# Query norms in the exponential and the maximum, halves of squares on GpSimd, one sine product per rotation

## The chip, the cores and the metric

The kernel runs on one core of a Trainium2 chip. The core has five engines that run their own instruction streams in order and meet at semaphores: TensorE (PE; PEld is its weight load), VectorE (DVE), ScalarE (ACT), GpSimd (POOL) and SyncE (SP), which issues the DMAs. The metric is the device time of one execution in microseconds (us), less is better. The median of three runs before the change is 3862.86 us.

## The reference

The reference is a network of two layers on 16 sequences of 256 tokens with 128 features. Each layer has a modulation, an attention and a feed-forward part. The part that matters here is the feed-forward of the first layer, which is itself a stack of six local attentions with gated networks between them. Cut down, one of the six attentions is:

```
q, k, v = split(shift_tokens(x) @ Wqkv)          # 16 heads of 64
q = q / max(norm(q), 1e-12) * q_scale            # per token and head
k = k / max(norm(k), 1e-12) * k_scale
q = q*cos*scale + rotate_half(q)*sin*scale       # rotate_half: [-second half, first half]
k = k*cos/scale + rotate_half(k)*sin/scale
sim = 8 * q @ k.T    over windows of 32 queries and their 64 keys, masked
out = softmax(sim) @ v ;  x = x + out @ Wo
```

The norm of a query is one number per token and head. It can be applied to the query, or later to the whole row of scores of that token and head.

## The kernel before, in words

The six attentions are in `local_layers` (line 498). The loop over the layers holds a software pipeline over units. A unit is half of a tile of 128 tokens: 128 tokens by 8 heads (HG = 8, so PR = 4 pairs of heads), 4 units per sequence, 64 per layer, 384 in all. Every engine has a function `slot(u)` that does, for the current unit and for the units that lag one to five behind it, its part in a fixed order that is written out by hand; `u.has(n)` and `u.par(n)` speak of the unit that lags by n. Nothing plans the order at run time: an engine that waits holds up all that stands behind it.

One slot does, by engine:

- TensorE: projects keys (into PSUM bank PJ[1]) and queries (PJ[0]) of unit u, each as three passes of split floats (`three_passes`, lines 45 to 47). Then it transposes rotated keys and queries of unit u-2 (L637, into TB and TA), multiplies by Wo for u-5 (L696), transposes the weights of u-3 (TB) and the outputs of u-4 (TA). Then it projects the values of u into PJ[0] again, which needs that the queries there are rotated (`values`, line 662). Last come the mask (L736) and the scores (L743) of u-2 and the products with the values of u-3 (L756).
- ScalarE: the square of the queries (L876), the keys and queries of u-2 out of PSUM (L904, L907), the square of the keys (L876), the transposed weights (L915), Ln and Exp for the inverse norms (L921, L925), the outputs (L930), the values (L886), and eight exponentials of 64 columns for u-2 (L893), whose bias is the negative maximum per token and head.
- VectorE: the rotation of the queries (L1035 by the cosines over all 64 columns, L1036 and L1037 by the sines over 32 columns each, which swap the halves), the residual (L1071), the rotation of the keys, a Newton step for the inverse norms of u-1 (L1054, L1056, L1061), the maximum of the scores (L1083), the reciprocal of the sums (L1088), the sum of the squares of 16 heads of 64 columns (L1043), the normalisation of the outputs (L1095), and the lower bound of the sums (L1049).
- GpSimd: splits the input where due (L1215, L1218), adds the two parts of the rotated queries (L1239), multiplies rotated keys and queries of u-1 by their inverse norms (L1233, keys first), adds the two parts of the rotated keys (L1248).
- SyncE: the DMAs that lay the values out for the windows.

The lines that count for what follows:

```
PE: wait k_ready(u-2); transposes keys;  wait q_ready(u-2); transposes queries
ACT: wait proj_done, sum_done(u-1); Square
DVE: wait sq_done; rotate;   sums: tensor_reduce(raw, sq[128 x 16 x 64]) -> sum_done
POOL: t1 = t1 + t2 (queries); t1 *= rn (keys) -> k_ready; t1 *= rn (queries) -> q_ready; t1 = t1 + t2 (keys)
```

Of the kernel before, what the change touches and what calls it, by code (L numbers as in the profile page):

```python
# [7 lines left out]
ALU = mybir.AluOpType  # L8
# [454 lines left out]
def wait_chunk(eng, sem, u, per, r):  # L463
# [9 lines left out]
    "ln_done", "guess_done", "newton", "qadd_done", "q_ready", "k_ready", "qk_done", "qk_out", "score_done",  # L473
# [24 lines left out]
def local_layers(nc, g, w, lw):  # L498
# [5 lines left out]
    with ExitStack() as ctx:  # L504
# [14 lines left out]
        t2 = sb("t2", [128, 2, 2, HG, HD])  # L519
        raw = sb("raw", [128, 2 * HG, 2])  # L520
# [10 lines left out]
        pT = sb("pT", [128, 2, PR, 128])  # L531
        nm = sb("nm", [128, 2, 2, PR])
# [19 lines left out]
        with nc.Block() as block:  # L552
# [81 lines left out]
            def _(pe):  # L634
# [31 lines left out]
                def front(u):  # L666
# [4 lines left out]
                    if u.has(2):  # L671
# [6 lines left out]
                        pe.wait_ge(s.q_ready, u.count(1, 2, 1))  # L678
# [187 lines left out]
            def _(act):  # L866
# [4 lines left out]
                def squares(u, j):  # L871

                    act.wait_ge(s.proj_done, u.count(3, 0, 2 - j))
                    if u.was(1):
                        act.wait_ge(s.sum_done, u.count(1, 1, 1))
# [13 lines left out]
                def slot(u):  # L889
                    def weights(e):  # L890

                        for p in range(PR):
                            last = nc.scalar.activation(pb[:, u.par(2), p, e, :], SC[:, e, p * KEYS:(p + 1) * KEYS],  # L893
                                                        ACT.Exp, bias=nm[:, u.par(2), e, p:p + 1])
                        last.then_inc(s.exp_done, 1)
# [105 lines left out]
            def _(dve):  # L1001
# [12 lines left out]
                def make_tables(made):  # L1014

                    for t in range(2):
                        nc.vector.tensor_tensor(ctab[:, t, :, :], g.cbase[:, t, :, :], scb[:, :, :], ALU.mult)
                        nc.vector.tensor_tensor(stab[:, t, :, 0:32], g.sbase[:, t, :, 0:32], scb[:, :, 32:64], ALU.mult)
                        last = nc.vector.tensor_tensor(stab[:, t, :, 32:64], g.sbase[:, t, :, 32:64],
# [6 lines left out]
                def rotate(u, j):  # L1026

                    b, T = u.par(0), u.tile(0)
                    one, two = slice(0, 32), slice(32, 64)
                    x = PJ[j][:, :].rearrange("p (h d) -> p h d", h=HG)  # L1030
                    table = lambda t, c: t[:, T, j, c].unsqueeze(1).broadcast_to((128, HG, c.stop - c.start))
                    dve.wait_ge(s.sq_done, u.count(2, 0, 1 + j))
                    if u.was(2):
                        dve.wait_ge(s.qk_done, u.count(2, 2, 2 - j))
                    nc.vector.tensor_tensor(t1[:, b, j], x, table(ctab, slice(0, HD)), ALU.mult)  # L1035
                    nc.vector.tensor_tensor(t2[:, b, j, :, one], x[:, :, two], table(stab, one), ALU.mult)  # L1036
                    nc.vector.tensor_tensor(t2[:, b, j, :, two], x[:, :, one], table(stab, two),  # L1037
                                            ALU.mult).then_inc(s.rot_done, 1)

                def sums(u):  # L1040
                    if u.was(1):
                        dve.wait_ge(s.ss_done, u.count(1, 1, 1))
                    nc.vector.tensor_reduce(raw[:, :, 0], sq[:, :, :], AX.X, ALU.add).then_inc(s.sum_done, 1)  # L1043
# [7 lines left out]
                def newton(u):  # L1051
# [7 lines left out]
                    if u.was(3):  # L1059
                        dve.wait_ge(s.q_ready, u.count(1, 3, 1))  # L1060
# [3 lines left out]
                def slot(u, between=None):  # L1064
# [144 lines left out]
            def _(pool):  # L1209
# [11 lines left out]
                def slot(u):  # L1221
# [8 lines left out]
                    def normalise(j):  # L1230

                        here = t1[:, u.par(1), j]
                        nc.gpsimd.tensor_tensor(here, here, rn[:, u.par(1), j * HG:(j + 1) * HG].unsqueeze(2).broadcast_to(  # L1233
                            (128, HG, HD)), ALU.mult).then_inc(s.k_ready if j else s.q_ready, 1)

                    b = u.par(0)
                    if u.has(0):
                        pool.wait_ge(s.rot_done, u.count(2, 0, 1))
                        nc.gpsimd.tensor_tensor(t1[:, b, 0], t1[:, b, 0], t2[:, b, 0], ALU.add).then_inc(s.qadd_done, 1)  # L1239
                    if u.has(1):  # L1240
                        pool.wait_ge(s.rn_done, u.count(1, 1, 1))
                        pool.wait_ge(s.kadd_done, u.count(1, 1, 1))
                        normalise(1)
                        pool.wait_ge(s.qadd_done, u.count(1, 1, 1))
                        normalise(0)
                    if u.has(0):
                        pool.wait_ge(s.rot_done, u.count(2, 0, 2))
                        nc.gpsimd.tensor_tensor(t1[:, b, 1], t1[:, b, 1], t2[:, b, 1], ALU.add).then_inc(s.kadd_done, 1)  # L1248
# [1342 lines left out]
```

## Time and profile before

| | us |
|---|---|
| median of 3 runs | 3862.86 |
| lowest and highest run | 3859.14 and 3867.37 |
| span of the profiled execution | 3862.6 |
| TensorE busy in it | 3675.0 (95%) |
| VectorE busy | 3134.3 (81%) |
| ScalarE busy | 2886.4 (75%) |
| GpSimd busy | 2453.8 (64%) |

The profiled execution has no time of its own beside its span; the span stands 0.3 us from the median of the runs. The chain of work that ended last, as the page gives it, covers only the last few microseconds of the program and tells nothing of the local attention. The busy shares come from one profiled execution and are averages over all stages of the program; the local attention runs from about 250 to 3220 us of the span, with the gated network between its layers. In the rows below, times of the timeline are counted from the start of the span, and a bracket says how long the engine was idle before the row and what released it.

### The profile page before, as it was taken

The numbers are of one execution on the slowest core, as the hardware profiler recorded it, in microseconds if no ns is written. First come the engines' busy times: TensorE is split into PE (matmuls) and PEld (weight loads), VectorE is DVE, ScalarE is ACT, GpSimd is POOL, SyncE is SP. The second block draws the span as 40 slices with busy tenths as digits, with TensorE's granted clock in tenths as the row PEclk, the third lists the DMA queues.
The fourth block names the chain that finished last, engine by engine and source line by source line (L and its number), as shares of the span: only waits on it lengthen the run. The fifth ranks groups of instructions, "written<-read, shape, count | busy, mean of one in ns | idle before, by whom it ended". The sixth has DMA issues, their size and how long they took to land. (4 is left out here: it accounts for less than half of the span.)

```text
span 3862.6 us, 189335 instructions
## 1 busy us (share of the span) xinstructions
PE 3675.0 (95%) x70910; PEld 2943.1 (76%) x70910; DVE 3134.3 (81%) x9407; ACT 2886.4 (75%) x8517; POOL 2453.8 (64%) x2556
## 2 busy tenths in 40 slices
PE   7869999999999999999999999999999999899997
PEld 4558888688886788876888868888688886466665
DVE  7878888688887788877888878888788887666667
ACT  5758888478885688866888758888478885677775
POOL 3657777377774677755777647777377773454553
PEclk8979999999999999999999999999999999899998
DMA  1013333233332233332333323333233331100000
GB/s 48 1 56 83 81 82 81 60 81 81 81 81 69 72 81 80 82 83 58 83 80 82 90 52 81 81 81 82 60 81 81 81 81 46 36 1 0 0 0 28
DMA packets 305289, 245.99 MB, mean 64 GB/s; under 512 B 74485, under 2 KB 299860, under 8 KB 304340
## 3 DMA queue, kind: packets, MB, share of 16 engines
q1 hardware_dynamic: 305108, 243.72, 25.0%
q8 instruction: 96, 1.57, 0.2%
q14 instruction: 85, 0.70, 0.1%
HBM read 24.54 MB, written 2.12 MB: 7 GB/s over the span
## 5 line engine op out<-in xcount | busy, mean ns | idle before, releaser
L1233 POOL TENSOR_TENSOR wa_t<-wa_t,wa_rn 128x512 f32<-128x512 f32 x768 | 785.4, 1043 | 280.5 <-DVE wa_rn L1061 277.0
L893 ACT ACTIVATE wa_pb<-wa_sc,wa_nm 128x64 f32<-128x64 f32 x3072 | 672.5, 330 | 365.1 <-DVE wa_nm L1083 340.1
L1239 POOL TENSOR_TENSOR wa_t<-wa_t 128x512 f32<-128x512 f32 x384 | 496.1, 1292 | 409.7 <-DVE wa_t L1037 409.6
L1035 DVE TENSOR_TENSOR wa_t<-wa_pj,wa_ctab 128x512 f32<-128x512 f32 x768 | 527.0, 686 | 210.5 <-PE wa_ta L637 137.6
L45 PE MATMUL wa_pj<-lw_wqkv_high,wa_xhigh 128*128 128x512 f32 x1152 | 532.7, 462 | 36.3 <-DVE wa_t L1037 17.7
L876 ACT ACTIVATE wa_sq<-wa_pj 128x512 f32<-128x512 f32 x768 | 487.5, 636 | 60.4 <-PE wa_pj L47 57.8
L1248 POOL TENSOR_TENSOR wa_t<-wa_t 128x512 f32<-128x512 f32 x384 | 490.1, 1276 | 0.0
L47 PE MATMUL wa_pj<-lw_wqkv_high,wa_xlow 128*128 128x512 f32 x1152 | 459.9, 399 | 0.0
L46 PE MATMUL wa_pj<-lw_wqkv_low,wa_xhigh 128*128 128x512 f32 x1152 | 457.6, 397 | 0.9 <-issue 0.9
L1043 DVE TENSOR_REDUCE wa_raw<-wa_sq 128x16 f32<-128x1024 f32 x384 | 448.9, 1169 | 0.0
L696 PE MATMUL wa_ob<-wa_oT,lw_wo 128*128 128x128 f32 x3120 | 419.7, 278 | 2.7 <-DVE wa_on L1095 2.6
L756 PE MATMUL wa_ob<-wa_vv,wa_pT 64*32 64x65 f32 x24576 | 388.5, 227 | 25.1 <-issue 22.5
L696 PEld LDWEIGHTS wa_ob<-wa_oT,lw_wo 128*128 128x128 f32 x3120 | 382.4, 193 | 7.0 <-issue 5.1
L756 PEld LDWEIGHTS wa_ob<-wa_vv,wa_pT 64*32 64x32 f32 x24576 | 317.7, 105 | 37.2 <-issue 28.3
L2215 POOL TENSOR_TENSOR mq_pb<-mq_pb,mq_rs 128x256 f32<-128x256 f32 (+1 forms) x256 | 206.2, 826 | 219.7 <-DVE mq_rs L2360 219.7
L743 PE MATMUL wa_sc<-wa_kT,wa_qT 64*32 64x64 f32 x24576 | 327.9, 223 | 1.9 <-issue 1.8
L1036 DVE TENSOR_TENSOR wa_t<-wa_pj,wa_stab 128x256 f32<-128x256 f32 x768 | 316.9, 413 | 0.0
L1037 DVE TENSOR_TENSOR wa_t<-wa_pj,wa_stab 128x256 f32<-128x256 f32 x768 | 316.8, 413 | 0.0
L743 PEld LDWEIGHTS wa_sc<-wa_kT,wa_qT 64*32 64x32 f32 x24576 | 300.3, 105 | 2.8 <-issue 2.4
L1083 DVE TENSOR_REDUCE wa_nm<-wa_sc 128x8 f32<-128x512 f32 x384 | 265.5, 691 | 44.8 <-PE wa_sc L743 22.0
L45 PEld LDWEIGHTS wa_pj<-lw_wqkv_high,wa_xhigh 128*128 128x128 f32 x1152 | 217.7, 189 | 107.5 <-DVE wa_t L1037 29.7
L1095 DVE TENSOR_TENSOR wa_on<-wa_ob,wa_rs 128x512 f32<-128x512 f32 x384 | 261.3, 681 | 1.5
(291 smaller groups left out, 8631.5 us busy)
## 6 DMA issues: line engine op xcount, KB each, us to landing
wa_vv<-wa_vt SPq DMA_DIRECT2D x2304, 65.0 KB
wa_vv<-wa_vt SPq DMA_DIRECT2D x1152, 32.5 KB
lw_wqkv<-L_ffn_Wqkv SPq DMA_DIRECT2D x6, 1536.0 KB, 6.2
lw_xs<-yT SPq DMA_DIRECT2D x96, 64.0 KB
lw_fs<-yT SPq DMA_DIRECT2D x48, 128.0 KB
lw_xs<-yT SPq DMA_DIRECT2D x96, 63.8 KB
lw_fs<-yT SPq DMA_DIRECT2D x96, 63.8 KB
lw_wo<-L_ffn_Wo SPq DMA_DIRECT2D x6, 512.0 KB, 4.1
```

The costliest lines, as they stand in the source:

```text
L45: nc.tensor.matmul(out, lhs[0], rhs[0], start=start, stop=False)
L46: nc.tensor.matmul(out, lhs[0], rhs[1], start=False, stop=False)
L47: return nc.tensor.matmul(out, lhs[1], rhs[0], start=False, stop=stop)
L696: last = nc.tensor.matmul(OB[:, 0, Y0:Y0 + 128], wo[:, PR * h + j, :], oT[:, u.tile(5), PR * h + j, :], start=(j == 0), stop=(j == PR - 1) ...
L743: last = nc.tensor.matmul(SC[q, e, p * KEYS:(p + 1) * KEYS], qT[r, u.par(2), p, q], kT[r, h2, p, k0:k0 + KEYS], start=False, stop=True, sk ...
L756: last = nc.tensor.matmul(OB[q, e, p * VW:(p + 1) * VW], pT[r, u.par(3), p, q], vv[r, u.ring(3), n, p, :], start=True, stop=True, skip_gro ...
L876: nc.scalar.activation(sq[:, j * HG:(j + 1) * HG, :], PJ[j][:, :].rearrange("p (h d) -> p h d", h=HG), ACT.Square).then_inc(s.sq_done, 1)
L893: last = nc.scalar.activation(pb[:, u.par(2), p, e, :], SC[:, e, p * KEYS:(p + 1) * KEYS], ACT.Exp, bias=nm[:, u.par(2), e, p:p + 1])
L1035: nc.vector.tensor_tensor(t1[:, b, j], x, table(ctab, slice(0, HD)), ALU.mult)
L1233: nc.gpsimd.tensor_tensor(here, here, rn[:, u.par(1), j * HG:(j + 1) * HG].unsqueeze(2).broadcast_to((128, HG, HD)), ALU.mult).then_inc(s. ...
L1239: nc.gpsimd.tensor_tensor(t1[:, b, 0], t1[:, b, 0], t2[:, b, 0], ALU.add).then_inc(s.qadd_done, 1)
L1248: nc.gpsimd.tensor_tensor(t1[:, b, 1], t1[:, b, 1], t2[:, b, 1], ALU.add).then_inc(s.kadd_done, 1)
```

## The change

Four things are changed, all in `local_layers`:

- The queries are no longer multiplied by their inverse norm. GpSimd's product for them goes, and with it the semaphore q_ready; TensorE waits for the addition (qadd_done) instead. The inverse norm now is the scale operand of the eight exponentials, and VectorE multiplies the negative maximum by it in an instruction of its own, after a wait for the maximum (peak_done).
- GpSimd adds the first and the second 32 squares of each head (into the new tile sh), and VectorE sums the 32 results instead of 64 squares. This addition stands first in GpSimd's slot, behind the split of the input; it waits for both squares of the unit, and signals half_done, for which the next squares and the sum wait.
- The rotation multiplies by the sines in one instruction of 64 columns, without the swap. The table of sines is laid out swapped for it.
- GpSimd's addition does the swap: two instructions of 32 columns per head in place of one of 64, for queries and for keys.

```diff
-                        pe.wait_ge(s.q_ready, u.count(1, 2, 1))
+                        pe.wait_ge(s.qadd_done, u.count(1, 2, 1))
...
-                        act.wait_ge(s.sum_done, u.count(1, 1, 1))
+                        act.wait_ge(s.half_done, u.count(1, 1, 1))
...
-                                                        ACT.Exp, bias=nm[:, u.par(2), e, p:p + 1])
+                                                        ACT.Exp, bias=nm[:, u.par(2), e, p:p + 1],
+                                                        scale=rn[:, u.par(2), 2 * p + e:2 * p + e + 1])
...
-                        nc.vector.tensor_tensor(stab[:, t, :, 0:32], g.sbase[:, t, :, 0:32], scb[:, :, 32:64], ALU.mult)
-                        last = nc.vector.tensor_tensor(stab[:, t, :, 32:64], g.sbase[:, t, :, 32:64],
+                        nc.vector.tensor_tensor(stab[:, t, :, 32:64], g.sbase[:, t, :, 0:32], scb[:, :, 32:64], ALU.mult)
+                        last = nc.vector.tensor_tensor(stab[:, t, :, 0:32], g.sbase[:, t, :, 32:64],
...
-                    nc.vector.tensor_tensor(t1[:, b, j], x, table(ctab, slice(0, HD)), ALU.mult)
-                    nc.vector.tensor_tensor(t2[:, b, j, :, one], x[:, :, two], table(stab, one), ALU.mult)
-                    nc.vector.tensor_tensor(t2[:, b, j, :, two], x[:, :, one], table(stab, two),
-                                            ALU.mult).then_inc(s.rot_done, 1)
+                    nc.vector.tensor_tensor(t1[:, b, j], x, table(ctab), ALU.mult)
+                    nc.vector.tensor_tensor(t2[:, b, j], x, table(stab), ALU.mult).then_inc(s.rot_done, 1)
...
-                    nc.vector.tensor_reduce(raw[:, :, 0], sq[:, :, :], AX.X, ALU.add).then_inc(s.sum_done, 1)
+                    dve.wait_ge(s.half_done, u.count(1, 0, 1))
+                    nc.vector.tensor_reduce(raw[:, :, 0], sh[:, :, :], AX.X, ALU.add).then_inc(s.sum_done, 1)
...
-                        dve.wait_ge(s.q_ready, u.count(1, 3, 1))
+                        dve.wait_ge(s.exp_done, u.count(2, 3, 2))
...
-                        nc.vector.tensor_reduce(nm[:, u.par(2), :, :], SC[:, :, 0:PR * KEYS].rearrange(
-                            "p e (a b) -> p e a b", a=PR), AX.X, ALU.max, negate=True).then_inc(s.mx_done, 1)
+                        nc.vector.tensor_reduce(mx[:, u.par(2), :, :], SC[:, :, 0:PR * KEYS].rearrange(
+                            "p e (a b) -> p e a b", a=PR), AX.X, ALU.max, negate=True).then_inc(s.peak_done, 1)
+                        dve.wait_ge(s.peak_done, u.count(1, 2, 1))
+                        nc.vector.tensor_tensor(nm[:, u.par(2), :, :], mx[:, u.par(2), :, :],
+                                                rn[:, u.par(2), 0:HG].rearrange("p (a e) -> p e a", e=2),
+                                                ALU.mult).then_inc(s.mx_done, 1)
...
+                    def turned(j):
+
+                        for to, of in ((one, two), (two, one)):
+                            here = t1[:, b, j, :, to]
+                            last = nc.gpsimd.tensor_tensor(here, here, t2[:, b, j, :, of], ALU.add)
+                        return last
+
                     if u.has(0):
+                        pool.wait_ge(s.sq_done, u.count(2, 0, 2))
+                        if u.was(1):
+                            pool.wait_ge(s.sum_done, u.count(1, 1, 1))
+                        nc.gpsimd.tensor_tensor(sh[:, :, :], sq[:, :, one], sq[:, :, two], ALU.add).then_inc(s.half_done, 1)
                         pool.wait_ge(s.rot_done, u.count(2, 0, 1))
-                        nc.gpsimd.tensor_tensor(t1[:, b, 0], t1[:, b, 0], t2[:, b, 0], ALU.add).then_inc(s.qadd_done, 1)
+                        turned(0).then_inc(s.qadd_done, 1)
                     if u.has(1):
                         pool.wait_ge(s.rn_done, u.count(1, 1, 1))
                         pool.wait_ge(s.kadd_done, u.count(1, 1, 1))
-                        normalise(1)
-                        pool.wait_ge(s.qadd_done, u.count(1, 1, 1))
-                        normalise(0)
+                        here = t1[:, u.par(1), 1]
+                        nc.gpsimd.tensor_tensor(here, here, rn[:, u.par(1), HG:2 * HG].unsqueeze(2).broadcast_to(
+                            (128, HG, HD)), ALU.mult).then_inc(s.k_ready, 1)
                     if u.has(0):
                         pool.wait_ge(s.rot_done, u.count(2, 0, 2))
-                        nc.gpsimd.tensor_tensor(t1[:, b, 1], t1[:, b, 1], t2[:, b, 1], ALU.add).then_inc(s.kadd_done, 1)
+                        turned(1).then_inc(s.kadd_done, 1)
```

## Rows read from the trace of the kernel before

**Rows 1.** The page: busy time, share of the span and instructions of each engine.

```profile
PE 3675.0 (95%) x70910; PEld 2943.1 (76%) x70910; DVE 3134.3 (81%) x9407; ACT 2886.4 (75%) x8517; POOL 2453.8 (64%) x2556
```

**Rows 2.** Windows: one stretch inside the local attention, busy us per engine, clock.

```profile
core 0: us, PE busy (x) PEld busy (x) DVE busy (x) ACT busy (x) POOL busy (x), PEclk, DMA share, GB/s
840.00:1160.00 320.00, 320.00 (x8152) 278.99 (x8158) 285.53 (x730) 273.43 (x829) 241.72 (x243) 1.00 0.33 81
```

**Rows 3.** The sum of squares, once per unit, in that stretch: min/median/max ns.

```profile
L1043 DVE TENSOR_REDUCE wa_raw<-wa_sq x49: 1165/1166/1170, 839.5 to 1155.3; 128x16 f32<-128x1024 f32 x49
```

**Rows 4.** Timeline of one unit: start, us, engine, line, out<-in, count, idle before.

```profile
902.61 0.49 PE L45 MATMUL wa_pj<-lw_wqkv_high,wa_xhigh 128*128 128x512 f32 x1
...
904.60 0.69 DVE L1083 TENSOR_REDUCE wa_nm<-wa_sc 128x8 f32<-128x512 f32 x1
...
905.33 1.75 ACT L893 ACTIVATE wa_pb<-wa_sc,wa_nm 128x64 f32<-128x64 f32 x8 [0.93 <-DVE wa_nm L1083]
...
906.28 0.59 PEld L637 LDWEIGHTS wa_tb<-ident,wa_t 128*128 128x128 f32 x4
...
906.92 0.65 ACT L876 ACTIVATE wa_sq<-wa_pj 128x512 f32<-128x512 f32 x1
...
907.66 0.69 DVE L1035 TENSOR_TENSOR wa_t<-wa_pj,wa_ctab 128x512 f32<-128x512 f32 x1 [0.48 <-ACT wa_sq L876]
...
908.27 0.41 DVE L1036 TENSOR_TENSOR wa_t<-wa_pj,wa_stab 128x256 f32<-128x256 f32 x1
...
908.35 0.68 ACT L876 ACTIVATE wa_sq<-wa_pj 128x512 f32<-128x512 f32 x1
908.60 0.41 DVE L1037 TENSOR_TENSOR wa_t<-wa_pj,wa_stab 128x256 f32<-128x256 f32 x1
...
909.07 0.49 PE L45 MATMUL wa_pj<-lw_wqkv_high,wa_xhigh 128*128 128x512 f32 x1
...
910.39 0.16 DVE L1054 TENSOR_TENSOR wa_rc<-wa_rg 128x16 f32<-128x16 f32 x1
910.58 0.18 DVE L1056 SCALAR_TENSOR_TENSOR wa_rc<-wa_rc,wa_ss 128x16 f32<-128x16 f32 x1
...
911.05 2.05 POOL L1233 TENSOR_TENSOR wa_t<-wa_t,wa_rn 128x512 f32<-128x512 f32 x2 [0.66 <-DVE wa_rn L1061]
...
911.68 1.75 ACT L893 ACTIVATE wa_pb<-wa_sc,wa_nm 128x64 f32<-128x64 f32 x8 [0.82 <-DVE wa_nm L1083]
...
912.87 0.59 PEld L637 LDWEIGHTS wa_tb<-ident,wa_t 128*128 128x128 f32 x4
```

**Rows 5.** Timeline near a layer's start: a square and the rotation that waited.

```profile
1284.22 0.65 ACT L876 ACTIVATE wa_sq<-wa_pj 128x512 f32<-128x512 f32 x1
...
1284.90 0.69 DVE L1035 TENSOR_TENSOR wa_t<-wa_pj,wa_ctab 128x512 f32<-128x512 f32 x1 [0.96 <-ACT wa_sq L876]
```

**Rows 6.** Waits over the whole program: us in total, times, longest us.

```profile
PEld wa_pj L45 <- DVE wa_t L1037: 29.7, 27, 2.9
...
PE wa_pj L45 <- issue: 12.2, 4, 3.3
```

**Rows 7.** ScalarE by form (total us, mean ns), and a timeline of four with both operands.

```profile
L915 ACT ACTIVATE wa_pT<-wa_tb 128x512 f32<-128x512 f32 x384 | 230.8, 601 | 26.0 <-PE wa_tb L637 18.7
L1540 ACT ACTIVATE la_col<-la_b,la_vec 128x512 f32<-128x512 f32 x24 | 16.5, 687 | 10.3 <-PE la_b L1438 10.3
L1582 ACT ACTIVATE la_row<-la_b,la_neg,la_rstd 128x128 f32<-128x128 f32 x32 | 12.0, 462 | 0.0
L1597 ACT ACTIVATE aT<-la_b,la_vec 128x512 f32<-128x512 f32 x8 | 6.2, 778 | 8.8 <-PE la_b L1429 8.8
...
124.51 1.50 ACT L1582 ACTIVATE la_row<-la_b,la_neg,la_rstd 128x128 f32<-128x128 f32 x4
```

**Rows 8.** GpSimd by form: total us and mean ns of one.

```profile
L1239 POOL TENSOR_TENSOR wa_t<-wa_t 128x512 f32<-128x512 f32 x384 | 496.1, 1292 | 409.7 <-DVE wa_t L1037 409.6
...
L1218 POOL TENSOR_TENSOR wa_xlow<-lw_xs,wa_xhigh 128x128 fp32r<-128x128 f32 x192 | 88.1, 459 | 15.0
```

More of the change, by code:

```diff
@@ L472 @@
     "xs_ready", "proj_done", "session", "sq_done", "ss_done", "sum_done", "rn_done", "rot_done",
-    "ln_done", "guess_done", "newton", "qadd_done", "q_ready", "k_ready", "qk_done", "qk_out", "score_done",
+    "ln_done", "guess_done", "newton", "qadd_done", "k_ready", "half_done", "peak_done", "qk_done", "qk_out", "score_done",
     "mx_done", "exp_done", "pT_done", "pT_out", "pv_done", "rs_done", "norm_done", "oT_done", "oT_out",
@@ L519, in local_layers @@
         t2 = sb("t2", [128, 2, 2, HG, HD])
+        sh = sb("sh", [128, 2 * HG, HD // 2])
         raw = sb("raw", [128, 2 * HG, 2])
@@ L531, in local_layers @@
         pT = sb("pT", [128, 2, PR, 128])
+        mx = sb("mx", [128, 2, 2, PR])
         nm = sb("nm", [128, 2, 2, PR])
@@ L1028, in rotate @@
                     b, T = u.par(0), u.tile(0)
-                    one, two = slice(0, 32), slice(32, 64)
                     x = PJ[j][:, :].rearrange("p (h d) -> p h d", h=HG)
-                    table = lambda t, c: t[:, T, j, c].unsqueeze(1).broadcast_to((128, HG, c.stop - c.start))
+                    table = lambda t: t[:, T, j, :].unsqueeze(1).broadcast_to((128, HG, HD))
                     dve.wait_ge(s.sq_done, u.count(2, 0, 1 + j))
@@ L1228, in slot @@
                         split_input(0, u.sequence(32, u.lead + 1, 32), u.sequence(4, u.lead + 1, 1))
[L1230 to L1234, printed above, removed]
                     b = u.par(0)
+                    one, two = slice(0, HD // 2), slice(HD // 2, HD)
+                    def turned(j):
[3 more added lines that the diff above has]
+                        return last
                     if u.has(0):
+                        pool.wait_ge(s.sq_done, u.count(2, 0, 2))
+                        if u.was(1):
+                            pool.wait_ge(s.sum_done, u.count(1, 1, 1))
+                        nc.gpsimd.tensor_tensor(sh[:, :, :], sq[:, :, one], sq[:, :, two], ALU.add).then_inc(s.half_done, 1)
                         pool.wait_ge(s.rot_done, u.count(2, 0, 1))
-                        nc.gpsimd.tensor_tensor(t1[:, b, 0], t1[:, b, 0], t2[:, b, 0], ALU.add).then_inc(s.qadd_done, 1)
+                        turned(0).then_inc(s.qadd_done, 1)
                     if u.has(1):
```

## The prediction, made before the changed kernel ran

> **What bounds the kernel now.** The first view is the table of engines on the page: TensorE is busy 95% of the span and VectorE 81% [rows 1]. The share of busy time averages over stages, so the second view is a stretch inside the local attention, 840 to 1160 us: TensorE is busy 320.00 of 320 us at full granted clock, while VectorE, ScalarE and GpSimd keep 10 to 25% idle [rows 2]. In that stretch one unit (128 tokens by 8 heads) takes (1155.3 - 839.5) / 48 = 6.58 us [rows 3], and there are 384 units, 2526 us of the 3862.6. So the question is what one unit costs.
>
> TensorE has no gap, but the reader must not stop there: all engines run in order, and a ring of work goes round once per unit beside TensorE's own queue. In the timeline of one unit [rows 4] it reads: TensorE begins the value projection V (902.61); scores follow, and VectorE begins their maximum at 904.60, 1.99 later; the eight exponentials begin at 905.33, 0.73 later; ScalarE, in order, begins the square of the next unit's queries at 906.92, 1.59 later; VectorE rotates those queries from 907.66, of which 0.65 is the square and 0.03 the hand-over (1284.22 + 0.65 = 1284.87, rotation at 1284.90 [rows 5]); the rotation ends at 908.60 + 0.41 = 909.01, 1.35 later; V of the next unit, which overwrites the queries' bank, begins at 909.07, 0.06 later. Necessary work in the ring: 1.99 + 0.73 + 1.59 + 0.68 + 1.35 + 0.06 = 6.40 us, against a period of 6.58. **The ring has only 0.18 us of slack.** Whatever is added to it beyond that is paid in every unit, however busy TensorE is; what is taken from VectorE outside it is worth nothing.
>
> **The change part by part.**
>
> *Reduction of squares.* The sum over 1024 columns (1.17 us, [rows 3]) becomes one over 512, about 0.63. It lies behind the reciprocal, in no link of the ring: VectorE gains 0.54 us of idleness per unit, which I price at nothing. Only where TensorE waits for a rotation (29.7 us in 27 places over the whole program [rows 6]) could an earlier VectorE show, and there too the queue in front of the rotation isn't the sum but the square.
>
> *Rotation.* Three products (start to start 0.60, 0.33, then 0.41 to its end, 1.35 in all) become two of 512 columns: 0.60 + 0.69 = 1.29. It is in the ring: -0.06.
>
> *Norm of queries in the maximum.* The maximum now goes to a tile of its own, then waits for its own semaphore, and a product of 8 columns makes the bias. No row has this product; the nearest is the chain of small operations in the Newton step, 910.39 to 910.58, 0.19 per link with its wait [rows 4]. Bounds: 0.10 (half a link) and 0.30 (one and a half). I take 0.19. The norm itself was made a unit earlier, so it isn't waited for. Queued behind on VectorE are the reciprocal, the sum and the normalisation, which have slack; who waits for it is ScalarE with the exponentials. In the ring: +0.19.
>
> *Norm of queries in the exponential.* Eight exponentials of 64 columns get a second operand per partition, the scale. Three rows of 512 columns from PSUM give its price: no such operand 0.601 us, bias alone 0.687, bias and scale 0.778 [rows 7], so the scale adds 0.091. That is the duration of one; what matters is the distance of starts. Now it is (1.75 - 0.33) / 7 = 0.203 us. With both operands on 128 columns from PSUM, four in a row take 1.50 us with 0.462 each: (1.50 - 0.462) / 3 = 0.346 [rows 7]. From 128 to 64 columns comes off what the columns cost: (0.778 - 0.462) / 384 = 0.82 ns each, 0.053 us. So 0.293 with both, and 8 x 0.293 = 2.34 against 1.59 before: +0.75. Bounds: 0 (the operand's read hides behind the seven neighbours) and 8 x 0.13 = 1.0. I take the duration's own difference, 8 x 0.091 = +0.73, since it needs no step from 128 to 64 columns.
>
> The Trainium skill, "ScalarE: Activation LUTs", section "What ACT_TABLE_LOAD costs", says that each per-partition pointer operand adds about 93 ns to an ACTIVATE and that neighbours overlap by about 93 ns. The first agrees with the 0.091 of the rows and would make the term 0.74 and the sum 4106 us. The second would put today's starts 0.24 apart, where the trace has 0.203; the measurement decides.
>
> *GpSimd.* Removed: the product of the query norm, 1.00 from start to start. Added: the halves of the squares, 512 columns, 1.25. The two additions of 1.27 become four of 256 columns; the rows have 0.459 at 128 and 1.292 at 512 [rows 8], so some 0.74 each, 0.70 from start to start. Per unit: 1.25 + 4 x 0.70 + 1.00 = 5.05, and with the split of the input 5.5 on average and 6.0 at most: below the period, so its load doesn't bind. Its order might: the key norm now stands behind the half addition, which waits for both squares. Square of keys to its end, +0.06, +1.25, +1.40, +1.04: keys are ready 3.75 after it; today it was 909.03, which gives 912.78 against TensorE's need at 912.87 [rows 4]. In the longer ring the key square ends 0.08 after V begins (V - 0.06 - 1.29 - 0.03 + 1.46), the keys are ready at V + 3.83 and TensorE asks at V + 3.80: late by hundredths, in front of a stretch in which TensorE waits 0.68 for the rotation anyway. Price nothing; with halves that don't shrink (1.29 each) it would be the bound, see below. The queries, on the other hand, are ready over 3 us earlier, which nobody waits for.
>
> **The sum.** New ring: 1.99 + 0.73 + 0.19 + (1.59 + 0.73) + 0.68 + 1.29 + 0.06 = 7.26 us. It passes the 6.58 of TensorE's queue, so the period becomes 7.26, +0.68. Not all 384 units pay: the first few of each layer stand in stalls of other causes (projections that wait up to 3.3 us for TensorE's own issue [rows 6]) and the last few have no next unit to square. I take 58 of 64, an estimate: 6 x 58 x 0.68 = 237, and 0.9 us longer once per layer at its end, of which half is hidden, 3. Span 3862.6 + 240 = 4103. The median of the runs, 3862.86, stands within 0.3 us of the profiled span, so nothing is converted: **4103 us**, 6% slower. TensorE is late next: it waits 0.68 us per unit for the rotation, some 9% of the loop.
>
> **Rivals.**
>
> 1. *The scale costs nothing between neighbours.* For it: neighbours overlap already by 0.13 each. Against: the 0.346 with both operands, also between neighbours. Ring 7.26 - 0.73 = 6.53, under 6.58, so TensorE's queue stays the bound: 3860, no change.
>
> 2. *Faster, by VectorE's relief.* Same condition, decided at a scaled start distance of at most 0.203 + (6.58 - 6.53) / 8 = 0.21 us; then VectorE's 0.6 us of new idleness can reach the 27 places where TensorE waits for a rotation. Price at most 29.7: 3833. Against it is the same row as above, and that those waits follow the squares.
>
> 3. *The scale costs about half* (starts 0.245 apart): ring 6.90, +0.32, 348 x 0.32 = 111: 3974. For it: sharing of the two operand reads; no row shows it.
>
> 4. *GpSimd becomes the bound.* The ring over two units through the key square, half addition, keys, transposes, V and exponentials is, from the weight load of the key transposes to V 906.28 to 909.07, 2.79; to the maximum 1.99; to the exponentials 0.92; to the next square 2.32; to the key square's end 906.92 to 909.03, 2.11; to the keys 3.75: 13.88 us, 6.9 per unit. From 1.0 us per half addition on it passes 7.26, and from 1.14 on GpSimd's own load does. With 1.29 each that load is 1.25 + 5.0 + 1.0 + 0.43 = 7.7 per unit: 348 x 1.1 = 383, 4245 us. Against: 459 ns at 128 columns shows that cost falls with the columns; for: rows of 32 columns with gaps are in no row.
>
> **How the numbers follow.** Forecast 0.79 (its own range 4050 to 4150, from the bounds 0.10 and 0.30 of the small product, and 0.27 to 0.31 of the start distance); rival 4 with its milder forms 0.08; rival 3 0.05; rival 1 0.04; rival 2 0.04. The range reaches 3990 to 4175, which leaves out the two rivals without the operand's cost and the outer part of 3 and 4. A measurement of this kernel can tell about 0.2% from no change; so faster 0.05, same 0.04, slower 0.91.
>
> **What would show it.** In the profile after: exponentials of some 420 ns, eight of them in 2.4 to 2.5 us instead of 1.75; unit period 7.2 to 7.3; TensorE with about 0.6 to 0.7 us of idleness per unit, in front of V or of the transposes just before it, released by the rotation or by ScalarE; ScalarE's idleness before the exponentials reduced; the sum near 0.63 us and much more idleness on VectorE; GpSimd halves of 0.7 us. The forecast is wrong if exponentials stay near 0.2 apart, if the period is set by the wait for GpSimd's keys, or if TensorE's granted clock, 1.00 in the loop, falls because of the new gaps.

## The result and the profile after

The changed kernel takes 4538.45 us (median of 4 runs, 4535.65 to 4540.83) against 3864.08 us (4 runs, 3859.14 to 3867.37): a ratio of 1.1747, 95% interval 1.1731 to 1.1764. It is 17.5% slower. The prediction had the sign, 4103 us and a range up to 4175: it saw little more than a third of the loss. Of the executions reported below, three were in a slower state (one of g1_dummy512 at 5691 us, two of g2_dummy_memset at 7034 and 8564) and enter no ratio.

The page of the kernel after, its engines and two of its costliest groups, against [rows 1]; the last row is the group of the exponentials before:

```profile
span 4538.8 us, 189966 instructions
...
PE 3865.4 (85%) x70910; PEld 2896.4 (64%) x70910; DVE 3412.0 (75%) x9023; ACT 3122.3 (69%) x8517; POOL 2648.0 (58%) x3324
...
L895 ACT ACTIVATE wa_pb<-wa_sc,wa_nm,wa_rn 128x64 f32<-128x64 f32 x3072 | 949.1, 414 | 836.7 <-DVE wa_nm L1087 836.7
...
L1242 POOL TENSOR_TENSOR wa_t<-wa_t 128x256 f32<-128x256 f32 x1536 | 1087.5, 730 | 0.0
...
L893 ACT ACTIVATE wa_pb<-wa_sc,wa_nm 128x64 f32<-128x64 f32 x3072 | 672.5, 330 | 365.1 <-DVE wa_nm L1083 340.1
```

ScalarE's exponentials waited 837 us for the bias, against 340 before. The odd number is VectorE's: 3412 us busy against 3134 before, though the columns of its sum were halved and its rotation has one instruction less. The groups of VectorE by form say where, total us and mean ns of one:

```profile
L1057 DVE SCALAR_TENSOR_TENSOR wa_rc<-wa_rc,wa_ss 128x16 f32<-128x16 f32 x384 | 245.2, 639 | 13.2
L1044 DVE TENSOR_REDUCE wa_raw<-wa_sh 128x16 f32<-128x512 f32 x384 | 241.9, 630 | 0.0
L1062 DVE SCALAR_TENSOR_TENSOR wa_rn<-wa_rc,wa_rg 128x16 f32<-128x16 f32 x384 | 233.9, 609 | 21.3
L1087 DVE TENSOR_TENSOR wa_nm<-wa_mx,wa_rn 128x8 f32<-128x8 f32 x384 | 193.6, 504 | 13.2
...
L1055 DVE TENSOR_TENSOR wa_rc<-wa_rg 128x16 f32<-128x16 f32 x384 | 85.1, 222 | 10.9 <-ACT wa_rg L928 10.9
```

The sum is 0.63 us as forecast. But two products of the Newton step, on 16 columns, have grown from 0.18 us in [rows 4] to 0.64 and 0.61, and the new product of 8 columns takes 0.50. The timeline of one unit shows what they have in common (compare [rows 4]):

```profile
1008.59 1.28 POOL L1249 TENSOR_TENSOR wa_sh<-wa_sq 128x512 f32<-128x512 f32 x1 [3.31 <-ACT wa_sq L878]
...
1009.71 0.20 DVE L1055 TENSOR_TENSOR wa_rc<-wa_rg 128x16 f32<-128x16 f32 x1
1009.83 1.42 POOL L1242 TENSOR_TENSOR wa_t<-wa_t 128x256 f32<-128x256 f32 x2
1009.94 0.65 DVE L1057 SCALAR_TENSOR_TENSOR wa_rc<-wa_rc,wa_ss 128x16 f32<-128x16 f32 x1
...
1010.72 0.56 DVE L1062 SCALAR_TENSOR_TENSOR wa_rn<-wa_rc,wa_rg 128x16 f32<-128x16 f32 x1
...
1011.20 0.68 DVE L1084 TENSOR_REDUCE wa_mx<-wa_sc 128x8 f32<-128x512 f32 x1
1011.36 1.04 POOL L1256 TENSOR_TENSOR wa_t<-wa_t,wa_rn 128x512 f32<-128x512 f32 x1
...
1011.91 0.51 DVE L1087 TENSOR_TENSOR wa_nm<-wa_mx,wa_rn 128x8 f32<-128x8 f32 x1
...
1012.36 1.41 POOL L1242 TENSOR_TENSOR wa_t<-wa_t 128x256 f32<-128x256 f32 x2
...
1012.46 2.47 ACT L895 ACTIVATE wa_pb<-wa_sc,wa_nm,wa_rn 128x64 f32<-128x64 f32 x8 [2.22 <-DVE wa_nm L1087]
...
1016.06 0.68 DVE L1038 TENSOR_TENSOR wa_t<-wa_pj,wa_stab 128x512 f32<-128x512 f32 x1
...
1016.93 0.48 PE L45 MATMUL wa_pj<-lw_wqkv_high,wa_xhigh 128*128 128x512 f32 x1
```

L1057 begins at 1009.94 and ends at 1010.59; GpSimd's first half addition began at 1009.83 and lasts 0.73, to 1010.56. L1062 ends at 1011.28; the second half addition ended at 1011.24. L1087 ends at 1012.42; the key norm ended at 1012.40. Each of the long VectorE instructions ends 0.02 to 0.04 us after a GpSimd instruction. Counted over all 384 units: L1057 begins while GpSimd runs in 373 and then takes 0.653 us (median), and 0.175 in the other 11; L1062 0.650 in 366 and 0.175 in 18; L1087 0.510 in 378 and 0.168 in 6. The reduction L1044, the rotations and L1100, which have at most one input in SBUF, keep their durations.

### The profile page after: what moved, and what is told of

It reads as the page before. It is cut to its first block and busy times, and to the rows that moved or that the text cites. A ratio compares the mean times of both kernels' runs of the same rounds, so it can differ in the third digit from the quotient of the medians.

```text
span 4538.8 us, 189966 instructions
## 1 busy us (share of the span) xinstructions
PE 3865.4 (85%) x70910; PEld 2896.4 (64%) x70910; DVE 3412.0 (75%) x9023; ACT 3122.3 (69%) x8517; POOL 2648.0 (58%) x3324
## 5 line engine op out<-in xcount | busy, mean ns | idle before, releaser
L895 ACT ACTIVATE wa_pb<-wa_sc,wa_nm,wa_rn 128x64 f32<-128x64 f32 x3072 | 949.1, 414 | 836.7 <-DVE wa_nm L1087 836.7
L1249 POOL TENSOR_TENSOR wa_sh<-wa_sq 128x512 f32<-128x512 f32 x384 | 494.2, 1287 | 1091.4 <-ACT wa_sq L878 1091.4
L1242 POOL TENSOR_TENSOR wa_t<-wa_t 128x256 f32<-128x256 f32 x1536 | 1087.5, 730 | 0.0
L639 PE MATMUL wa_tb<-ident,wa_pb 128*128 128x128 f32 x1536 | 247.2, 284 | 383.0 <-ACT wa_kT L907 380.9
L1038 DVE TENSOR_TENSOR wa_t<-wa_pj,wa_stab 128x512 f32<-128x512 f32 x768 | 522.0, 680 | 0.0
L639 PEld LDWEIGHTS wa_tb<-ident,wa_pb 128*128 128x128 f32 x1536 | 162.3, 141 | 448.8 <-ACT wa_kT L907 226.2
L1256 POOL TENSOR_TENSOR wa_t<-wa_t,wa_rn 128x512 f32<-128x512 f32 x384 | 400.9, 1044 | 71.3 <-DVE wa_rn L1062 30.1
L758 PE MATMUL wa_ob<-wa_vv,wa_pT 64*32 64x65 f32 x24576 | 348.0, 228 | 29.5 <-issue 26.2
L758 PEld LDWEIGHTS wa_ob<-wa_vv,wa_pT 64*32 64x32 f32 x24576 | 284.3, 105 | 33.7 <-issue 32.6
L1084 DVE TENSOR_REDUCE wa_mx<-wa_sc 128x8 f32<-128x512 f32 x384 | 260.5, 678 | 1.2 <-PE wa_sc L745 0.8
L1100 DVE TENSOR_TENSOR wa_on<-wa_ob,wa_rs 128x512 f32<-128x512 f32 x384 | 259.3, 675 | 1.5
```

What stands on the lines that cost most here:

```text
L758: last = nc.tensor.matmul(OB[q, e, p * VW:(p + 1) * VW], pT[r, u.par(3), p, q], vv[r, u.ring(3), n, p, :], start=True, stop=True, skip_gro ...
L1038: nc.vector.tensor_tensor(t2[:, b, j], x, table(stab), ALU.mult).then_inc(s.rot_done, 1)
L1242: last = nc.gpsimd.tensor_tensor(here, here, t2[:, b, j, :, of], ALU.add)
L1249: nc.gpsimd.tensor_tensor(sh[:, :, :], sq[:, :, one], sq[:, :, two], ALU.add).then_inc(s.half_done, 1)
```

## The experiments

**Theory A.** A VectorE instruction whose two tensor inputs both lie in SBUF doesn't get through while a GpSimd instruction with SBUF inputs runs; it waits for that instruction's end. (A tile lies in SBUF or in PSUM; the kernel makes the first by `sb` and the second by `ps`.) **Rival B.** The products are long for a reason of VectorE's own (semaphores, code, order). A third theory, for the other part of the loss, is the prediction's: the scale operand costs 0.73 us per unit in the ring.

All runs in one table: the links of the ring of the prediction, us, each a mean over 228 units (38 in the loop of each of the six layers), worked out from the timelines; then the median time and its ratio to before. V is the start of TensorE's value projection; the columns follow the ring from there to the next V. In VectorE's order the Newton step stands right in front of the maximum, so a Newton product that is held shows in "V to max", and the product of the maxima shows in "to exp".

| kernel | V to max | to exp | to square | to rotation | rotation | to V | period | time | ratio |
|---|---|---|---|---|---|---|---|---|---|
| before | 2.00 | 0.73 | 1.65 | 0.77 | 1.35 | 0.08 | 6.58 | 3864 | 1 |
| predicted ring | 1.99 | 0.92 | 2.32 | 0.68 | 1.29 | 0.06 | 7.26 | 4103 | |
| after | 2.74 | 1.26 | 2.32 | 0.69 | 1.29 | 0.15 | 8.45 | 4538 | 1.175 |
| f1_rc_psum | 2.22 | 1.12 | 2.32 | 0.69 | 1.29 | 0.15 | 7.80 | 4309 | 1.116 |
| f2_mx_psum | 2.74 | 0.92 | 2.32 | 0.69 | 1.29 | 0.15 | 8.12 | 4418 | 1.144 |
| f3_both_psum | 2.22 | 0.93 | 2.33 | 0.69 | 1.29 | 0.15 | 7.62 | 4238 | 1.097 |
| f4_scale0 | 2.75 | 1.26 | 1.59 | 0.70 | 1.29 | 0.15 | 7.74 | 4266 | 1.105 |
| e4_order | 1.92 | 1.15 | 2.32 | 0.69 | 1.29 | 0.15 | 7.52 | 4197 | 1.087 |
| f6_order_mx | 1.91 | 0.94 | 2.33 | 0.69 | 1.29 | 0.15 | 7.31 | 4129 | 1.068 |
| f7_order_mx_scale0 | 1.98 | 0.94 | 1.59 | 0.71 | 1.29 | 0.14 | 6.65 | 3885 | 1.005 |
| e6_norm_only | 1.91 | 1.15 | 2.32 | 0.69 | 1.35 | 0.10 | 7.53 | 4213 | 1.091 |
| e7_half_only | 2.87 | 0.72 | 1.59 | 0.72 | 1.35 | 0.09 | 7.34 | 4133 | 1.071 |
| e8_sine_only | 1.99 | 0.73 | 1.66 | 0.77 | 1.29 | 0.14 | 6.57 | 3857 | 0.999 |
| g1_dummy512 | 2.94 | 0.72 | 1.59 | 0.72 | 1.35 | 0.08 | 7.42 | 4155 | 1.075 |
| g2_dummy_memset | 2.00 | 0.73 | 1.65 | 0.77 | 1.35 | 0.08 | 6.58 | 3863 | 1.000 |

### Where the inputs lie

**f1_rc_psum**: the Newton step's tile in PSUM.

```diff
-                    b = u.par(1)
+                    b, rc = u.par(1), rs_tail if u.tail else PJ[1][:, 0:16]
+                    if not u.tail:
+                        dve.wait_ge(s.rot_done, u.count(2, 0, 2))
...
+                    if u.was(2):
+                        pe.wait_ge(s.rn_done, u.count(1, 2, 1))
                     project(u, PJ[1], 1)
```

> The kernel after, with the Newton step's small tile rc in PSUM (in the keys' bank, free by then) instead of SBUF; all instructions and their order stay. Theory A (a VectorE instruction with two SBUF inputs waits until GpSimd's running instruction ends): the two Newton products that read rc fall from 0.64 and 0.61 us to about 0.2 each, since they now read one SBUF tile. The maximum starts 0.6 us earlier, but its product then falls on GpSimd's key norm (1.04 us) and waits for nearly all of it, so that the unit keeps all but 0.1 to 0.2 us: 4470 to 4510 us, and the product grows from 0.50 to 0.9 to 1.0 us. Rival B (the long products are the engine's own, from semaphores, code or the order of the work): the products stay at 0.6 us, 4538 us or a little more.

Measured: 4308.66 us, ratio 1.116 (1.1141 to 1.1179). The two products that now read one SBUF tile fell to 0.18 and 0.17 us: theory A, not B. (In a layer's last unit the tile stays in SBUF; 378 of 384 units read PSUM.) The time fell by 230 us, much more than expected, because the product of the maxima didn't grow to 0.9 us but shrank, from 504 to 370 ns on the mean. Two units show how:

```profile
1005.53 1.43 POOL L1247 TENSOR_TENSOR wa_t<-wa_t 128x256 f32<-128x256 f32 x2
1005.67 0.18 DVE L1062 SCALAR_TENSOR_TENSOR wa_pj<-wa_pj,wa_ss 128x16 f32<-128x16 f32 x1
...
1005.89 0.17 DVE L1067 SCALAR_TENSOR_TENSOR wa_rn<-wa_pj,wa_rg 128x16 f32<-128x16 f32 x1
...
1006.75 0.23 DVE L1092 TENSOR_TENSOR wa_nm<-wa_mx,wa_rn 128x8 f32<-128x8 f32 x1
...
1006.90 1.06 POOL L1261 TENSOR_TENSOR wa_t<-wa_t,wa_rn 128x512 f32<-128x512 f32 x1
...
1014.11 1.06 POOL L1261 TENSOR_TENSOR wa_t<-wa_t,wa_rn 128x512 f32<-128x512 f32 x1
1014.58 0.61 DVE L1092 TENSOR_TENSOR wa_nm<-wa_mx,wa_rn 128x8 f32<-128x8 f32 x1
```

In the first, the product L1092 asked at 1006.75, while the second half addition ran, and got through at 1006.98, when that ended: the key norm L1261, next in GpSimd's queue, did not keep it out. So it is held by the instruction that is running, at most one, and not by GpSimd's queue. This happens in 179 units (mean 0.22 us). In the second, it asked 0.47 us after the key norm had begun and was held to that one's end, as I had expected of all; this happens in 199 units (mean 0.51). The first Newton product, both inputs of which are the same SBUF tile rg, is still held up by the first half addition in 198 units (0.71 us) and not in the others (0.18; mean of all 0.46). It writes to PSUM here, so it isn't its writing that is kept out.

**f2_mx_psum**: the maxima in PSUM.

```diff
-        mx = sb("mx", [128, 2, 2, PR])
+        mx = SC[:, 0, 256:272].rearrange("p (b e a) -> p b e a", b=2, e=2)
```

> The kernel after, with the tile of maxima in PSUM (spare columns of the scores' bank) instead of SBUF; nothing else. Theory A: the product of the maxima falls from 0.50 to about 0.2 us, the Newton products stay at 0.6: 0.3 us less per unit, 4538 - 348 x 0.3 = 4434 us (4410 to 4450). Rival B: the product stays near 0.5 us, 4538 us.

Measured: 4417.58 us, ratio 1.1442 (1.1423 to 1.1461). The product fell from 504 to 167 ns and the link from 1.26 to 0.92; the Newton products stayed at 639 and 610 ns. As theory A had it.

**f3_both_psum**: both edits together.

> The kernel after, with both tiles in PSUM. Theory A: all three products near 0.2 us, V to maximum back from 2.65 to 2.0 and maximum to exponentials from 1.26 to 0.93: 1.0 us less per unit, a period of 7.5 and 4538 - 348 x 1.0 = 4190 us (4120 to 4230); more than the two changes alone together. Rival B: no change, 4538 us.

Measured: 4238.0 us, ratio 1.0973 (1.0955 to 1.0991). Of theory A's 350 us 300 came. What is missing lies in the first Newton product, with its one tile as both inputs:

```profile
1008.05 1.41 POOL L1247 TENSOR_TENSOR wa_t<-wa_t 128x256 f32<-128x256 f32 x2
1008.13 0.70 DVE L1060 TENSOR_TENSOR wa_pj<-wa_rg 128x16 f32<-128x16 f32 x1
...
1008.86 0.18 DVE L1062 SCALAR_TENSOR_TENSOR wa_pj<-wa_pj,wa_ss 128x16 f32<-128x16 f32 x1
...
1009.42 1.05 POOL L1261 TENSOR_TENSOR wa_t<-wa_t,wa_rn 128x512 f32<-128x512 f32 x1
...
1010.11 0.17 DVE L1092 TENSOR_TENSOR wa_nm<-wa_sc,wa_rn 128x8 f32<-128x8 f32 x1
```

L1060 began at 1008.13, 0.08 behind the start of a half addition, and lasted to 1008.83; V to maximum is 2.22, not 2.0. That product reads the same tile twice and is held like the others. L1092 runs through the key norm L1261 in 0.17 us.

### When GpSimd runs

**e4_order**: GpSimd's key norm ahead of the additions for the queries, so that it idles during the Newton step.

```diff
-                        pool.wait_ge(s.rot_done, u.count(2, 0, 1))
-                        turned(0).then_inc(s.qadd_done, 1)
                     if u.has(1):
...
                     if u.has(0):
                         pool.wait_ge(s.rot_done, u.count(2, 0, 2))
+                        turned(0).then_inc(s.qadd_done, 1)
                         turned(1).then_inc(s.kadd_done, 1)
```

> The kernel after, with GpSimd's key norm moved ahead of the additions for the queries; all instructions stay. Theory A (a VectorE instruction with two SBUF inputs waits for the end of GpSimd's running one): GpSimd now idles until the Newton step is done, so its last two products fall to 0.18 us and V to maximum from 2.74 to 2.0; the product of the maxima still meets the key norm, 0.45 to 0.5 us. Period 8.45 - 0.8 = 7.65, 4538 - 348 x 0.8 = 4260 us (4230 to 4290). Rival B (GpSimd's order doesn't matter to VectorE, only what VectorE runs itself): 4538 us. Rival C (GpSimd's longer chain was the bound): slower than 4538 us or equal, since its work is the same.

Measured: 4196.54 us, ratio 1.0873 (1.0855 to 1.0892), 342 us less than after with the same instructions, and more than the 280 that were expected:

```profile
1007.07 0.17 DVE L1057 SCALAR_TENSOR_TENSOR wa_rc<-wa_rc,wa_ss 128x16 f32<-128x16 f32 x1
...
1007.28 0.18 DVE L1062 SCALAR_TENSOR_TENSOR wa_rn<-wa_rc,wa_rg 128x16 f32<-128x16 f32 x1
...
1007.47 0.69 DVE L1084 TENSOR_REDUCE wa_mx<-wa_sc 128x8 f32<-128x512 f32 x1
1007.54 1.04 POOL L1254 TENSOR_TENSOR wa_t<-wa_t,wa_rn 128x512 f32<-128x512 f32 x1 [0.53 <-DVE wa_rn L1062]
...
1008.19 0.41 DVE L1087 TENSOR_TENSOR wa_nm<-wa_mx,wa_rn 128x8 f32<-128x8 f32 x1
...
1008.54 2.80 POOL L1242 TENSOR_TENSOR wa_t<-wa_t 128x256 f32<-128x256 f32 x4
```

Newton's last two products take 0.17 us, GpSimd idle; the product of the maxima, 0.41, meets the end of the key norm (1007.54 + 1.04 = 1008.58, product's end 1008.60). B falls. C (GpSimd's chain is the bound) falls less surely by this run alone, since the new order also brings the keys sooner: TensorE waited 142 us in all for the key norm in the kernel after and 0.5 here. But f2_mx_psum left GpSimd's work and order alone and gained 121 us. V to maximum is 1.92 us where 2.0 was expected, which no run explains.

**g1_dummy512** and **g2_dummy_memset**: the kernel before, with one more instruction on GpSimd, whose result nobody uses, behind the addition for the queries.

```diff
                         nc.gpsimd.tensor_tensor(t1[:, b, 0], t1[:, b, 0], t2[:, b, 0], ALU.add).then_inc(s.qadd_done, 1)
+                        nc.gpsimd.tensor_tensor(dy[2][:, :], dy[0][:, :], dy[1][:, :], ALU.add)
```

> The kernel before plus one GpSimd addition of 512 columns of tiles that nobody uses, behind the addition for the queries; nobody waits for it but GpSimd's own queue. Theory A: the second Newton product waits for its end, 1.0 to 1.2 us instead of 0.175, as with the half addition; period 7.3, 4130 us (4080 to 4160). Rival B (only the half addition's own data and semaphores matter): Newton products stay at 0.175; GpSimd is free for 1.2 us more than it needs here, and the time stays at 3860 to 3900 us.

Measured: 4154.73 us, ratio 1.0746 (1.0725 to 1.0768). An instruction that nobody needs costs 292 us. The product that was held is the first of Newton, 1.20 us on the mean, not the second:

```profile
1003.00 1.28 POOL L1241 TENSOR_TENSOR wa_dy<-wa_dy 128x512 f32<-128x512 f32 x1
1003.04 1.26 DVE L1055 TENSOR_TENSOR wa_rc<-wa_rg 128x16 f32<-128x16 f32 x1
...
1004.34 0.17 DVE L1057 SCALAR_TENSOR_TENSOR wa_rc<-wa_rc,wa_ss 128x16 f32<-128x16 f32 x1
```

```diff
+                        nc.gpsimd.memset(dy[:, :], 0.0)
```

> The kernel before plus a GpSimd memset of 1024 columns at the same place, which reads nothing. Theory A1 (any running GpSimd instruction holds VectorE's two-input ones up): the Newton product that meets it is lengthened to the memset's end, and the time rises with it, by up to 0.18 us per unit less than the memset lasts. Theory A2 (only GpSimd instructions that read SBUF do): Newton products stay at 0.17 us, and the time at 3860 us (3850 to 3890). I hold A1 a little likelier, from the additions that were held to the very end of GpSimd's instruction.

Measured: 3862.84 us, ratio 0.9997 (0.9987 to 1.0008). The memset lasts 0.96 us and covers all three Newton products, and none is held:

```profile
1000.87 0.96 POOL L1241 MEMSET wa_dy<- 128x1024 f32 x1
...
1000.94 0.17 DVE L1055 TENSOR_TENSOR wa_rc<-wa_rg 128x16 f32<-128x16 f32 x1
1001.14 0.18 DVE L1057 SCALAR_TENSOR_TENSOR wa_rc<-wa_rc,wa_ss 128x16 f32<-128x16 f32 x1
...
1001.44 0.17 DVE L1062 SCALAR_TENSOR_TENSOR wa_rn<-wa_rc,wa_rg 128x16 f32<-128x16 f32 x1
```

I had held A1 a little likelier; A2 is right: a GpSimd instruction that only writes keeps nobody out, and the additions and products do. A memset also is another kind of instruction than an addition, and no run has one that reads a single input. Nor is reading SBUF enough; see the last section.

### The parts of the change alone

**e8_sine_only**, from the kernel before, only the single sine product and `turned(0)`, `turned(1)`.

> The kernel before with the single sine product and the swap in GpSimd's additions alone. By theory A the two halves of the queries' addition end 0.1 us later than one addition did, so that only the first Newton product waits for 0.1 to 0.2 us, which the ring's slack of 0.18 holds: no change, 3863 us (3850 to 3890). By the prediction's prices the same, 3860 us. Rival D (halves of 256 columns with gaps cost much more, or their reads disturb VectorE's): over 3950 us.

Measured: 3857.49 us, ratio 0.9992 (0.9982 to 1.0002): no change clear of noise. The first Newton product is at 0.22 us, the ring still within its slack.

**e7_half_only**, only the half addition, the sum over sh and half_done in place of sum_done:

> The kernel before with the halves of the squares alone. By theory A the half addition pushes GpSimd's query addition into the Newton step: its first product waits for some 1.1 us, the ring has 7.4 to 7.5 us against 6.40, 3862 + 348 x 0.9 = 4175 us (4100 to 4200). By the prediction's prices it costs nothing and VectorE gains 0.54 us of idleness: 3860 us.

Measured: 4133.32 us, ratio 1.0705 (1.0686 to 1.0724). This is the edit that I priced at nothing. It costs 270 us alone:

```profile
1003.33 1.29 POOL L1243 TENSOR_TENSOR wa_sh<-wa_sq 128x512 f32<-128x512 f32 x1 [0.16 <-ACT wa_sq L877]
...
1004.57 1.32 POOL L1245 TENSOR_TENSOR wa_t<-wa_t 128x512 f32<-128x512 f32 x1
1004.59 0.17 DVE L1056 TENSOR_TENSOR wa_rc<-wa_rg 128x16 f32<-128x16 f32 x1
1004.78 1.14 DVE L1058 SCALAR_TENSOR_TENSOR wa_rc<-wa_rc,wa_ss 128x16 f32<-128x16 f32 x1
```

The half addition pushes the query addition L1245 from before the Newton step into it (1004.57 to 1005.89), and L1058 is held until 1005.92. This happens in 321 of the 384 units; its mean is 1.02 us.

**e6_norm_only**, only the scale operand, the product of the maxima and the query norm off GpSimd:

> The kernel before with the query norm part alone (scale operand, product of the maxima, no query norm on GpSimd). By theory A GpSimd is idle in the Newton step as before, the product of the maxima meets the key norm (0.5 us): ring 2.0 + 1.26 + 2.32 + 0.68 + 1.35 + 0.06 = 7.67 us, 3862 + 348 x 1.09 = 4240 us (4210 to 4280). By the prediction's prices (product 0.19, no contention) 7.32: 4120 us. Rival: the scale isn't on the path here, under 4000 us.

Measured: 4213.45 us, ratio 1.0913 (1.0894 to 1.0931). The ring has 0.73 us of scale, 0.19 of the product itself and 0.23 of contention more, the product at 0.39 us.

### Closing the account

**f4_scale0**, the kernel after with a constant scale:

```diff
-                                                        ACT.Exp, bias=nm[:, u.par(2), e, p:p + 1],
-                                                        scale=rn[:, u.par(2), 2 * p + e:2 * p + e + 1])
+                                                        ACT.Exp, bias=nm[:, u.par(2), e, p:p + 1], scale=0.0)
```

> The kernel after, with the constant 0 as scale of the exponentials instead of the norm per partition; this leaves the query norm and the scores' values out of the weights. The scale operand costs 8 x 0.091 in the ring by the prediction: 0.7 us less per unit, 4538 - 348 x 0.7 = 4290 us (4270 to 4310), eight exponentials in 1.75 us. Rival (GpSimd's or TensorE's order sets the period): less than half of that, over 4400 us.

Measured: 4265.64 us, ratio 1.1051 (1.1032 to 1.1071), 273 us less; the link to the square went from 2.32 back to 1.59, by the 0.73 of the prediction. 4270 to 4310 us were expected. Like f7_order_mx_scale0 below, this kernel leaves the query norm and the scores' values out of the weights.

**f6_order_mx**, e4_order with f2_mx_psum's line, so the whole change without its collisions:

> The kernel after with the key norm ahead of the queries' additions on GpSimd, and the tile of maxima in PSUM: both collisions of theory A are gone and all four parts of the change remain. V to maximum 1.92, to the exponentials 0.93, to the square 2.32, 0.69, rotation 1.29, 0.15 to V: a period of 7.30 (the prediction had 7.26), so 3862 + 348 x 0.74 = 4120 us (4100 to 4140). If something else than these collisions and the scale operand costs, it stays above 4160 us.

Measured: 4128.7 us, ratio 1.068 (1.0662 to 1.0698), period 7.31. **This is as near as a run comes to what the prediction computed**, 7.26 and 4103 us: all four parts of the change, and no product held but the first of Newton, 0.22 us instead of 0.17. The agreement has some luck in it: V to maximum is 0.08 us shorter than predicted and "to V" 0.09 longer.

**f7_order_mx_scale0**, the same with the constant scale:

> The same with the constant 0 as scale of the exponentials, which leaves the query norm and the scores' values out of the weights: the ring falls by 0.73 to 6.57 us, level with TensorE's own queue, so 3860 to 3890 us, the time before. If the ring had another term that I haven't seen, it would stay over 3920 us.

Measured: 3884.88 us, ratio 1.0045 (1.0028 to 1.0062), period 6.65. So, taken out in this order, the collisions account for 410 us (4538 - 4129) and the scale operand for 244; 21 us are left, about the 0.07 us by which the ring's 6.65 stands over the 6.58 before. Taken out first, in f4_scale0, the scale operand is worth 273: the parts of the loss share the ring's slack and don't simply add.

No version beats the kernel before clear of noise; e8_sine_only is level with it.

## Why the prediction was wrong, step by step

What failed is the overlap. The prediction let VectorE's small products run beside GpSimd's additions at no cost, and so priced the half addition at nothing and the product of the maxima at 0.19 us. It missed by 435 us (4538 - 4103), and 410 of them are the collisions that f6_order_mx takes away.

- *What bounds the kernel* was right: the ring with 0.18 us of slack beside TensorE's queue. Every run's time follows its period (in the ten kernels with a period over 7, each us above 6.58 costs 346 to 368 us above 3864; the prediction took 348), and TensorE, 320 of 320 us busy in [rows 2], now has gaps for 16% of such a stretch, at full granted clock. Windows of after, busy us of each engine, clock, DMA:

```profile
900.00:1400.00 500.00, 420.59 (x9967) 330.66 (x9967) 390.58 (x824) 367.36 (x1003) 324.88 (x414) 1.00 0.26 63
```

- *The rotation*, 1.29 us, was right (1.29), and so was *the scale operand*: 8 exponentials in 2.47 us, distance to the square 2.32, the mean of one 414 ns.
- *The period's other links* were right where nothing collides. "To V" is 0.15 instead of 0.06: in some units V follows the transposes that wait for ScalarE's kT eviction, a branch of nearly the ring's length. In the unit above the rotation ended at 1016.06 + 0.68 = 1016.74, and V began at 1016.93; ahead of it TensorE had waited 0.99 us for that eviction. No run takes this branch apart.
- *The sum of the squares* failed: "in no link of the ring ... which I price at nothing". Its saving is in no link. But the half addition that buys it sits in GpSimd's queue and shifts what stands behind it by 1.25 us, into the Newton step. In the kernel after, VectorE was idle 1.2 us before the maximum L1084 in all 384 units together (44.8 in the kernel before): its own queue, Newton step included, now sets the start of the maximum, and the link that the prediction kept at 1.99 us is 2.74. e7_half_only, the half addition alone: 270 us.
- *The product of the maxima* was mis-sized: 0.19 with bounds 0.10 and 0.30 from the Newton links of [rows 4]. It measured 0.53 (1.26 against 0.73), of which 0.34 is the wait for GpSimd (f2_mx_psum). The row that I took as nearest, L1056 at 910.58, was one in which GpSimd was idle, as in all 384 units before, and I didn't ask that of it.
- *GpSimd* failed in the same way: I priced its load and its order towards TensorE ("Its order might"), its halves rightly (0.70 from start to start forecast, 0.69 measured), and not whom it keeps out while it runs. The queries' halves hold Newton's last two products, 0.90 us together on the mean (639 and 609 ns against 175 each). The keys, forecast late by hundredths, made TensorE wait 0.37 us per unit (142 us in all); in the unit above the 0.99 us for the kT eviction come behind that wait and ahead of V, so it shows in no link.
- The range left all of this out, since none of its rivals was contention. It could be read before, not in [rows 2] but in two groups of one form in the trace of the kernel before:

```profile
L1967 DVE TENSOR_TENSOR m_hid_low<-m_hid,m_hid_high 128x512 fp32r<-128x512 f32 x64 | 50.2, 833 | 21.7 <-ACT m_hid_high L1954 21.4
...
L1135 DVE TENSOR_TENSOR gm_xlow<-gm_xnT,gm_xhigh 128x512 fp32r<-128x512 f32 x48 | 32.7, 682 | 4.3 <-ACT gm_xhigh L952 4.3
```

Both subtract two SBUF tiles. For L1967 the median is 679 ns in the 51 cases in which GpSimd was idle at its start, and 1512 in the 13 in which it ran. Two rows of one form with different means asked for a reason.

The Trainium skill states the rule that the prediction lacked. "SBUF — State Buffer", section "SBUF: two separate sides", calls the port pair that VectorE and GpSimd share "an **exclusive lock**, not a bandwidth split": a VectorE instruction with two SBUF inputs and a GpSimd instruction that reads SBUF exclude each other for the whole instruction, whichever starts first. The runs agree for VectorE and give the size: from 0.175 to 0.65 us under additions of 0.73, 1.26 under one of 1.28 (g1_dummy512), and 0.17 under the memset, which reads nothing. They agree the other way round too: a GpSimd subtraction that began under L1967 took 1.61 us instead of 1.27 to 1.36. They don't agree for a GpSimd power of 4 columns, which reads two SBUF tiles, lasts 1.01 us and kept L1135 out in none of 36 cases (rows below); there the measurement decides.

## What to carry to other kernels

Before work is moved to GpSimd, list VectorE's instructions with two SBUF inputs and see in the timeline whether GpSimd adds or multiplies at their time: a product of 16 columns then lasts as long as what is left of GpSimd's instruction. What took the collisions away here is GpSimd's order (342 us), and one of the two inputs in PSUM (230 and 121 us). And a scale per partition in many small activations is charged once for each of them, 0.09 us times eight in every unit, if they stand in the ring that sets the period.

## What the runs showed of the hardware that I had not expected

- A held VectorE instruction gets in when GpSimd's running instruction ends, ahead of GpSimd's next (f1_rc_psum: asked at 1006.75, done at 1006.98, with the key norm queued). VectorE's small products leave GpSimd's durations as they are: 730 ns for a half addition, 1.28 us for the whole one. A long one doesn't. In the kernel before, GpSimd's subtraction L2011 takes 1.61 to 1.63 us in the 5 cases in which it begins while VectorE's subtraction L1967 runs, and 1.27 to 1.36 in the other 9:

```profile
168.11 1.06 DVE L1967 TENSOR_TENSOR m_hid_low<-m_hid,m_hid_high 128x512 fp32r<-128x512 f32 x1 [0.39 <-ACT m_hid_high L1954]
168.70 1.61 POOL L2011 TENSOR_TENSOR m_x_low<-aT,m_x_high 128x512 fp32r<-128x512 f32 x1
...
183.49 1.35 POOL L2011 TENSOR_TENSOR m_x_low<-aT,m_x_high 128x512 fp32r<-128x512 f32 x1
```

- Not every GpSimd instruction that reads SBUF holds VectorE. In 36 of its 48 cases before, L1135, with two SBUF inputs, begins while GpSimd raises 4 columns to a power (L1278, 1.01 us) and keeps its 0.68 us; 36 of 48 again in the kernel after. It begins some 0.3 to 0.5 us after the power; no run shows whether one that begins sooner is held.

```profile
710.80 1.01 POOL L1278 TENSOR_TENSOR gm_rstd<-gm_rstd,mhalf 128x4 f32<-128x4 f32 x1
711.14 0.68 DVE L1135 TENSOR_TENSOR gm_xlow<-gm_xnT,gm_xhigh 128x512 fp32r<-128x512 f32 x1
```

- Two reads of the same SBUF tile count as two inputs (rg times rg: 1.20 us on the mean in g1_dummy512). One SBUF and one PSUM input don't (0.17 us in f2_mx_psum, 0.18 and 0.17 in f1_rc_psum, with GpSimd running).
- GpSimd's memset of 1024 columns, 0.95 us, holds nobody up.
